# Attention expansions in two row groups and two banks, with a new bank plan for the eight slots

## The chip, the cores and the metric

The kernel is one program on one core of a Trainium2 chip. Its time is the device time of one execution in microseconds (us); less is better. The engines are TensorE (PE in the profile, with PEld for its weight loads), VectorE (DVE), ScalarE (ACT), GpSimd (POOL) and the queue that issues transfers (SP). PE writes only to PSUM, which has eight banks of 128 partitions by 512 fp32 columns; DVE and ACT read PSUM, POOL does not. Engines wait for each other by semaphores.

## The reference

```python
x = L0_attn_hidden_states                      # 16 x 256 x 128
x = x + 0.5 * ffn(layernorm(x))
x = x + retention(layernorm(x))
x = x + 0.5 * ffn(layernorm(x))

def ffn(src):                                  # 16 heads of 8 dimensions, 4 experts of 512
    q, k, v = src @ Wq + bq, src @ Wk + bk, src @ Wv + bv
    scores = einsum("bqhd,bkhd->bhqk", q, k) * 8 ** -0.5
    attn = einsum("bhqk,bkhd->bqhd", softmax(scores), v).reshape(B, T, 128) @ Wo + bo
    x = layer_norm(src + attn, ln1_g, ln1_b)
    expert_idx = remainder(floor(x @ router_w + router_b), 4)
    ff_out = W2[e] @ relu(W1[e] @ x + b1[e]) + b2[e] for the expert e of each token
    return layer_norm(x + ff_out, ln2_g, ln2_b)
```

The changed part is the attention inside `ffn`, which runs twice over 16 batch elements of 256 tokens.

## The kernel before

The program has five stages in a row: attention of the first `ffn`, its experts, the retention layer, attention of the second `ffn` (whose first iterations are woven into the last ones of retention), its experts. At the start a DMA also clears two DRAM tables of 17.5 MB each, into which POOL later writes rows (`sort_out`).

**An attention iteration `i`** (one batch element enters in each) is cut into eight slots, p = 0 to 7; every engine runs its own list of work slot by slot, written out by hand, and semaphores tie the lists together. A slot begins on PE with `score_burst`: eight matmuls that contract over 32 rows each (array shape 32*128 in the profile). Four are the scores of two heads of element `i` (line 540, into `score_duo`, banks 0 and 1), four are the shifted scores of two heads of an earlier group (line 546, into `prob_duo`, banks 2 and 3). Within a burst neighbours take different row groups and banks. DVE then takes the row maxima of `score_duo` (`maximum`, line 1251) and ACT the exponential of `prob_duo` (`exp`, line 970). There is one `score_duo` and one `prob_duo`, so the next burst waits for both (`max_done`, `exp_done`).

Behind the burst each slot has other work on PE:

- **expand(b, g)**, lines 526 to 535: 16 heads of 8 dimensions lie in four groups of 4 heads, that is 32 of the 128 partitions. An expansion spreads a group's query and key rows, kept as a rounded part `qk_hi` and a remainder `qk_lo`, into a stack of 32 rows for each head, by matmuls with 0/1 selectors `sel_r`. ACT copies query and key half to SBUF (`out_expand`, lines 955 and 956, about 0.38 and 0.48 us).
- **spread_max(b, g)**: adds the maxima to the query stack (lines 578, 580); ACT copies it (`shift_q`, line 962).
- **weigh_values(b, g)**: probabilities times values (line 596, array shape 128*32, 16 matmuls in the profile) into `pv_bank`, two groups side by side; ACT copies (`out_pv`, line 978).
- **att_to_tokens, att_to_dims, project_out**: transposes (605, 613) and the output projection (621), with `normalize` on DVE (1260, 1262), `out_attT` on ACT (985) and `add_attention` on DVE (1270) between them.
- **transposes, project_qk, project_v** for elements to come; DVE makes `qk_lo` (`split_qk`, line 1240).
- **position(b)**: small bf16 matmuls for the row numbers of the experts' table (630 to 633); DVE reads them in `place`.

Four banks serve all of this: `pv_bank` (bank 4) and the three rotating banks `a`, `b`, `c` (5, 6, 7). `take(which, reader, value)` waits until the last reader of that bank has finished and notes the next one. In the profile and in the order below a pair of banks is one tensor: duo2 is banks 4 and 5, duo3 is 6 and 7.

## Time and profile before

| | |
|---|---|
| median of 3 runs | 1073.31 us (1070.42 to 1078.86) |
| the profiled execution, device time | 1071.67 us |
| its span in the trace | 1069.9 us (1.8 us lie around it) |
| PE busy | 891.4 us, 83% |
| DVE busy | 761.7 us, 71% |
| ACT busy | 687.3 us, 64% |
| POOL busy | 618.9 us, 58% |
| first attention | about 13 to 310 us |
| experts | about 310 to 400 us |
| retention | about 400 to 670 us |
| second attention | about 670 to 960 us |
| experts | 960 to 1070 us |

Busy shares are means over stages with different limits. In a timeline row the first number is the start in us from the span's beginning, the second the time covered by the row's instructions, and brackets at the end give the idle time of that engine before it and what ended it; a row without brackets follows its predecessor closely. A matmul's row begins with the weight load that it needs, if nothing hides that.

### The profile page before, as it was taken

What the parts mean: (1) busy time and instruction counts of PE and PEld (TensorE: products, weight loads), DVE (VectorE), ACT (ScalarE), POOL (GpSimd) and SP (SyncE); (2) the same over time, 40 slices, a digit from 0 to 9 for tenths busy, and PEclk for the clock granted to TensorE, in tenths of its full rate; (3) what the DMA queues carried; (4) which work ended last, traced back from release to release, by engine and by line L of the source; (5) the groups of instructions that cost most, each with busy time, mean ns of one, the idle gap of its engine ahead of it and who ended that gap; (6) DMA issues with size and microseconds to landing.
All of it is one profiled execution on the core that took longest, in us unless ns stands there. A gap on an engine that the chain in (4) does not pass through costs nothing. (4 is left out here: it accounts for less than half of the span.)

```text
span 1069.9 us, 26869 instructions
## 1 busy us (share of the span) xinstructions
PE 891.4 (83%) x8603; PEld 662.6 (62%) x8603; DVE 761.7 (71%) x1900; ACT 687.3 (64%) x1402; POOL 618.9 (58%) x913
## 2 busy tenths in 40 slices
PE   5898999999957883788888888799999999975884
PEld 4566666666636883566666665666666666644884
DVE  4687888888864874465555655578888888873776
ACT  2586888888835772344343434488888888853764
POOL 4144657566572774366657666426575665652666
PEclk9898999999988996799999999799999999996998
DMA  9984991000017773000000000000000000006772
GB/s 307 411 328 56 367 405 45 10 20 10 21 36 216 245 221 94 1 1 1 0 0 0 0 0 1 1 2 12 11 20 10 20 15 15 22 20 195 213 215 89
DMA packets 41958, 97.70 MB, mean 91 GB/s; under 512 B 5240, under 2 KB 25486, under 8 KB 37276
## 3 DMA queue, kind: packets, MB, share of 16 engines
q1 hardware_dynamic: 36380, 84.16, 23.9%
q0 software_dynamic: 5504, 12.63, 3.3%
q8 instruction: 37, 0.61, 0.2%
q14 instruction: 37, 0.30, 0.1%
HBM read 44.68 MB, written 53.13 MB: 91 GB/s over the span
## 5 line engine op out<-in xcount | busy, mean ns | idle before, releaser
L1251 DVE TENSOR_REDUCE mx<-duo 128x4 fp32r<-128x1024 f32 x256 | 312.4, 1220 | 74.3 <-PE duo L540 69.4
L970 ACT ACTIVATE probs<-duo 128x1024 f32<-128x1024 f32 x256 | 263.2, 1029 | 54.1 <-PE duo L546 50.6
L540 PE MATMUL duo<-stacks 32*128 32x256 f32 x1024 | 133.7, 338 | 32.9 <-DVE mx L1251 26.8
L596 PE MATMUL duo<-probs,v_st 128*32 128x256 f32 x2048 | 140.9, 394 | 0.9 <-ACT probs L970 0.6
L1473 DVE TENSOR_TENSOR ret<-duo,dm 128x768 f32<-128x768 f32 x64 | 61.2, 957 | 104.2 <-PE duo L785 100.4
L546 PE MATMUL duo<-q_st,stacks 32*128 32x256 f32 x1024 | 131.2, 335 | 0.1
L540 PEld LDWEIGHTS duo<-stacks 32*128 32x128 f32 x1024 | 80.7, 191 | 68.9 <-issue 39.0
L1625 POOL TENSOR_TENSOR a_ln<-mv_ln,eps_ln 128x2 f32<-128x2 f32 x32 | 6.4, 199 | 145.8 <-DVE mv_ln L1216 145.8
L533 PE MATMUL duo<-qk_hi,sel_r 128*128 128x256 f32 x256 | 83.3, 345 | 7.4 <-DVE qk_lo L1240 7.4
L596 PEld LDWEIGHTS duo<-probs,v_st 128*32 128x32 f32 x2048 | 54.3, 111 | 42.2 <-issue 3.4
L546 PEld LDWEIGHTS duo<-q_st,stacks 32*128 32x128 f32 x1024 | 77.8, 188 | 1.4 <-ACT probs L970 0.5
L1678 POOL DMA_INDIRECT x_sorted<-rows,pos_all x64 | 66.2, 1034 | 19.0 <-issue 19.0
L677 PE MATMUL duo<-w,probs 128*128 x608 | 76.4, 280 | 0.4 <-issue 0.2
L677 PEld LDWEIGHTS duo<-w,probs 128*128 128x128 f32 x608 | 73.5, 197 | 0.8 <-issue 0.8
L1082 ACT ACTIVATE stacks<-duo 128x512 fp32r<-128x512 f32 x64 | 38.2, 598 | 54.7 <-PE duo L797 54.7
L962 ACT ACTIVATE q_st<-duo 128x256 fp32r<-128x256 f32 x128 | 49.6, 387 | 33.7 <-PE duo L580 33.7
L534 PE MATMUL duo<-qk_lo,sel_r 128*128 128x256 f32 x256 | 69.9, 293 | 0.0
L533 PEld LDWEIGHTS duo<-qk_hi,sel_r 128*128 128x128 f32 x256 | 50.9, 199 | 23.4 <-DVE qk_lo L1240 12.0
L956 ACT ACTIVATE stacks<-duo,small 128x256 fp32r<-128x256 f32 x128 | 61.8, 483 | 0.0
L1001 ACT ACTIVATE probs<-duo,wside 128x256 f32<-128x256 f32 x152 | 60.0, 470 | 1.8 <-PE duo L668 1.6
L1774 POOL TENSOR_TENSOR qk<-att_un 128x512 f32<-128x512 f32 x16 | 20.3, 1271 | 63.8 <-DVE att_un L1486 63.8
L955 ACT ACTIVATE stacks<-duo 128x256 fp32r<-128x256 f32 x128 | 49.2, 384 | 8.4 <-PE duo L534 8.2
(213 smaller groups left out, 2423.4 us busy)
## 6 DMA issues: line engine op xcount, KB each, us to landing
x_sorted<-ret SPq DMA_DIRECT2D x2, 17476.0 KB, 52.8
wbuf<-w_pack SPq DMA_DIRECT2D x38, 512.0 KB, 3.4
ret<-x_sorted SPq DMA_DIRECT2D x22, 257.0 KB, 3.5
stacks<-x_sorted SPq DMA_DIRECT2D x12, 257.0 KB, 3.7
wside<-w_pack SPq DMA_DIRECT2D x38, 66.0 KB, 4.0
w_pack<-wbuf SPq DMA_DIRECT2D x2, 1024.0 KB, 7.8
decay_rows<-prow SPq DMA_DIRECT2D x1, 1536.0 KB
probs<-x_sorted SPq DMA_DIRECT2D x4, 257.0 KB, 4.3
```

The source lines that it names most:

```text
L533: pe.matmul(half, sel_r[:, g, 2 * n, :], qk_hi[:, n, :], start=True, stop=False)
L534: last = pe.matmul(half, sel_r[:, g, 2 * n + 1, :], qk_lo[:, n, :], start=False, stop=True)
L540: return pe.matmul(score_bank[h % 2][:, t * SEQ:(t + 1) * SEQ], q_st[r:r + 32, g, t * P:(t + 1) * P], k_st[r:r + 32, g, :], start=True, st ...
L546: return pe.matmul(banks[h % 2][:, t * SEQ:(t + 1) * SEQ], k_st[r:r + 32, g, t * P:(t + 1) * P], q2_st[r:r + 32, g, :], start=True, stop=True)
L596: last = pe.matmul(pv_bank[32 * j:32 * j + 32, cols], v_st[:, t, h, :], probs[:, h % RING, t, :], start=(t == 0), stop=(t == TT - 1))
L677: last = pe.matmul(bank[4 + n % 2][:, t * P:(t + 1) * P], hid[:, n % 2, c, t * P:(t + 1) * P], w2[:, bass.ds(e * CPE + c, 1), :], start=(c ...
L956: act.activation(k_st[:, g, :], o[:, SEQ:2 * SEQ], ACT.Identity, bias=ones_col[:]).then_inc(ex_ready, 1)
L970: act.activation(probs[:, h % RING:h % RING + 2, :, :], duo_now[:].rearrange("p (n t q) -> p n t q", n=2, t=TT), ACT.Exp, scale=SCALE).the ...
L1001: act.activation(hid[:, n % 2, c, :], bank[c][:, 0:SEQ], ACT.Relu, bias=wside[:, n % 3, c:c + 1]).then_inc(h_ready, 1)
L1251: dve.tensor_reduce(rows, score_duo[:].rearrange("p (n t k) -> p n t k", n=2, t=TT), AX.X, ALU.max, negate=True).then_inc(max_done, 1)
L1473: dve.tensor_tensor(ret[:, 2 * g:2 * g + 2, :], both, dm[:, 2 * g:2 * g + 2, :], ALU.mult).then_inc(ret_ready, 1)
L1678: pool.indirect_dma_start(x_sorted[b // BATCH], bass.IndirectOffsetOnAxis(pos_all[:, b - base, t:t + 1], 0), rows[:, b - base, t, :], None ...
```

## The change

`expand` uses only the 32 rows of its group instead of all 128. Queries lie in row group g, keys (whose weight columns and bias are rolled by 32 on the host, and the key selectors with them) in row group g + 1, so that query and key matmuls can be in the array at once; they now write to different banks, query to `a`, key to `c`. The count of matmuls is the same, four for each expansion. `pv_bank` becomes a rotating bank `d`. `position` moves from slot 4 to slot 5, `att_to_dims` from slot 0 to slot 1, `place` steps one slot later. Which bank the other work takes is redone.

The core of the diff (left out are the same edits of `turn` at the start of a phase, and the packing of `vecs`):

```diff
-                        sel[p, g, kind, 32 * j + HD * part + d] = 1.0
+                        sel[(p + 32 * (kind // 2)) % P, g, kind, 32 * j + HD * part + d] = 1.0
...
+    A["Wk"], A["bk"] = np.roll(A["Wk"], 32, 1), np.roll(A["bk"], 32)
...
-                return {"a": bank_a, "b": bank_b, "c": bank_c}[which]
+                return {"a": bank_a, "b": bank_b, "c": bank_c, "d": pv_bank}[which]
...
-                o = take("caac"[g], ex_ready, b * 8 + 2 * g + 2)
-                for n in range(2):
-                    half = o[:, n * SEQ:(n + 1) * SEQ]
-                    pe.matmul(half, sel_r[:, g, 2 * n, :], qk_hi[:, n, :], start=True, stop=False)
-                    last = pe.matmul(half, sel_r[:, g, 2 * n + 1, :], qk_lo[:, n, :], start=False, stop=True)
+                o = take("a", ex_ready, b * 8 + 2 * g + 1), take("c", ex_ready, b * 8 + 2 * g + 2)
+                for m, part in enumerate((qk_hi, qk_lo)):
+                    for n in range(2):
+                        r = 32 * ((g + n) % GROUPS)
+                        last = pe.matmul(o[n][:, 0:SEQ], sel_r[r:r + 32, g, 2 * n + m, :], part[r:r + 32, n, :], start=(m == 0), stop=(m == 1))
...
-                o = take("aaca"[g], q2_ready, b * 4 + g + 1)
+                o = take("acac"[g], q2_ready, b * 4 + g + 1)
...
-                if g == 0:
-                    pe.wait_ge(va_ready, b + 1)
-                    wait(pe, un_ready, b * 2)
-                if g == 2:
-                    pe.wait_ge(vb_ready, b + 1)
-                    pe.wait_ge(un_ready, b * 2 + 1)
+                if g % 2 == 0:
+                    pe.wait_ge((va_ready, vb_ready)[g // 2], b + 1)
+                    take("d", un_ready, b * 2 + g // 2 + 1)
...
-                o = take("ba"[t], att_ready, b * 2 + t + 1)
+                o = take("db"[t], att_ready, b * 2 + t + 1)
...
-                o = take("c", attT_ready, b + 1)
+                o = take("a", attT_ready, b + 1)
...
-                o = take("c", y1_ready, b + 1)
+                o = take("d", y1_ready, b + 1)
...
-                            if live(i - 2, base):
-                                att_to_dims(i - 2)
                         elif p == 1:
                             if live(i - 1, base):
                                 weigh_values(i - 1, 1)
+                            if live(i - 2, base):
+                                att_to_dims(i - 2)
+                            if live(i - 1, base):
                                 spread_max(i - 1, 3)
...
                             if live(i - 1, base):
                                 weigh_values(i - 1, 2)
+                        elif p == 5:
                             if live(i - 3, base):
                                 position(i - 3)
-                        elif p == 5:
```

On PE, in slots 4 and 5 of an iteration with all its parts. Before, from the expansion behind the burst of slot 4 to the burst of slot 5:

```order
L533 MATMUL duo3<-qk_hi,sel_r 128x256 [waits y1_ready]
L534 MATMUL duo3<-qk_lo,sel_r 128x256
L533 MATMUL duo3<-qk_hi,sel_r 128x256
L534 MATMUL duo3<-qk_lo,sel_r 128x256
L596 MATMUL duo2<-probs,v_st 32x256 [waits un_ready,vb_ready,exp_done]
L596 MATMUL duo2<-probs,v_st 32x256 x7
L630 MATMUL duo2<-masks,tri_b 128x8 [waits q2_ready,router]
L631 MATMUL duo2<-masks,ones_b 128x4
L633 MATMUL duo2<-counts,ones_b 128x8 x2
L540 MATMUL duo0<-stacks 128x256 [waits exp_done,q2_ready,max_done]
```

The same place in the change, on to the small matmuls of `position` (now line 628) and the values of slot 5:

```order
L535 MATMUL duo2<-qk_hi,sel_r 128x256 [waits ex_ready,q2_ready]
L535 MATMUL duo3<-qk_hi,sel_r 128x256
L535 MATMUL duo2<-qk_lo,sel_r 128x256
L535 MATMUL duo3<-qk_lo,sel_r 128x256
L594 MATMUL duo2<-probs,v_st 32x256 [waits y1_ready,vb_ready,exp_done]
L594 MATMUL duo2<-probs,v_st 32x256 x7
L541 MATMUL duo0<-stacks 128x256 [waits exp_done,q2_ready,max_done]
L541 MATMUL duo0<-stacks 128x256
L547 MATMUL duo1<-q2_st,stacks 128x256 x2
L541 MATMUL duo0<-stacks 128x256 x2
L547 MATMUL duo1<-q2_st,stacks 128x256 x2
L628 MATMUL duo2<-masks,tri_b 128x8 [waits ex_ready,router]
```

The four matmuls of the expansion alternate between the two banks, and `position` stands behind the burst of slot 5, where it waits for ACT's query copy of slot 4 (`ex_ready`) instead of for `q2_ready`.

On DVE, in slots 5 and 6. Before, from the maxima of slot 5 to those of slot 6, with the row numbers' first step just ahead:

```order
L1314 TENSOR_TENSOR pos_f<-duo2,masks 128x8 [waits pos_ps]
L1251 TENSOR_REDUCE mx<-duo0 128x2x2 [waits score_ps,prep_ln]
L1240 SCALAR_TENSOR_TENSOR qk_lo<-duo3,bias_cols,qk_hi 128x256 [waits ex_ps,hi_ready]
L1240 SCALAR_TENSOR_TENSOR qk_lo<-duo3,bias_cols,qk_hi 128x256
L1318 TENSOR_REDUCE pos_all<-pos_f 128x2 [waits pos_ready]
L1320 TENSOR_TENSOR counts<-counts,masks 128x8
L1216 BN_AGGR mv_prep<-six_prep 128x2 x2
L1251 TENSOR_REDUCE mx<-duo0 128x2x2 [waits m_ps,score_ps]
```

In the change:

```order
L1254 TENSOR_REDUCE mx<-duo0 128x2x2 [waits score_ps,prep_ln]
L1317 TENSOR_TENSOR pos_f<-duo2,masks 128x8 [waits pos_ps]
L1243 SCALAR_TENSOR_TENSOR qk_lo<-duo3,bias_cols,qk_hi 128x256 [waits ex_ps,hi_ready]
L1243 SCALAR_TENSOR_TENSOR qk_lo<-duo3,bias_cols,qk_hi 128x256
L1219 BN_AGGR mv_prep<-six_prep 128x2 x2
L1254 TENSOR_REDUCE mx<-duo0 128x2x2 [waits m_ps,score_ps]
L1263 RECIPROCAL rsum<-duo2 128x16 [waits attT_ps,att_ps]
L1265 TENSOR_TENSOR att_pair<-duo2,rsum 128x128 [waits rsum_ready]
L1321 TENSOR_REDUCE pos_all<-pos_f 128x2 [waits pos_ready]
L1323 TENSOR_TENSOR counts<-counts,masks 128x8
```

The first step of the row numbers comes behind the maxima of slot 5 and ahead of `split_qk`; the other two come behind `normalize` in slot 6.

On ACT, in slots 0 and 1. Before:

```order
L956 ACTIVATE stacks<-duo2,small 128x256
L948 ACTIVATE v_nat<-duo3 128x256 [waits vb_ready,v_ps]
L985 ACTIVATE att_pair<-duo3 128x256 [waits wo_ps,attT_ps]
L970 ACTIVATE probs<-duo1 128x1024 [waits pv_done,prob_ps]
L978 ACTIVATE att_un<-duo2 128x512 [waits att_ps,pv_done]
L962 ACTIVATE q2_st<-duo2 128x256 [waits prob_ps,m_ps]
```

In the change:

```order
L958 ACTIVATE stacks<-duo3,small 128x256
L951 ACTIVATE v_nat<-duo3 128x256 [waits vb_ready,v_ps]
L972 ACTIVATE probs<-duo1 128x1024 [waits pv_done,prob_ps]
L980 ACTIVATE att_un<-duo2 128x512 [waits att_ps,pv_done]
L987 ACTIVATE att_pair<-duo2 128x256 [waits wo_ps,attT_ps]
L964 ACTIVATE q2_st<-duo3 128x256 [waits prob_ps,m_ps]
```

The copy of `att_to_dims` leaves slot 0 and stands in slot 1, ahead of the copy of the shifted queries.

## Rows read from the trace of the kernel before

**Rows 1.** The page, part 2: granted TensorE clock, tenths, 40 slices of the span.

```profile
PEclk9898999999988996799999999799999999996998
```

**Rows 2.** Busy time in stretches: PE, PEld, DVE, ACT, POOL with counts, PEclk, DMA.

```profile
114.00:131.00 17.00, 15.89 (x186) 11.05 (x187) 15.00 (x35) 14.54 (x28) 11.07 (x18) 1.00 1.03 413
...
898.00:915.00 17.00, 15.87 (x193) 10.98 (x185) 14.90 (x34) 14.59 (x28) 11.06 (x18) 1.00 0.04 15
```

**Rows 3.** Timeline, DVE: the maxima of slots 3 to 7 and 0 to 3.

```profile
239.65 1.21 DVE L1251 TENSOR_REDUCE mx<-duo 128x4 fp32r<-128x1024 f32 x1
...
241.92 1.23 DVE L1251 TENSOR_REDUCE mx<-duo 128x4 fp32r<-128x1024 f32 x1 [0.21 <-DVE six_ln L1210]
...
243.94 1.23 DVE L1251 TENSOR_REDUCE mx<-duo 128x4 fp32r<-128x1024 f32 x1 [0.27 <-PE duo L540]
...
246.16 1.19 DVE L1251 TENSOR_REDUCE mx<-duo 128x4 fp32r<-128x1024 f32 x1
...
248.09 1.23 DVE L1251 TENSOR_REDUCE mx<-duo 128x4 fp32r<-128x1024 f32 x1 [0.26 <-PE duo L540]
...
250.21 1.23 DVE L1251 TENSOR_REDUCE mx<-duo 128x4 fp32r<-128x1024 f32 x1 [0.40 <-PE duo L540]
...
252.39 1.22 DVE L1251 TENSOR_REDUCE mx<-duo 128x4 fp32r<-128x1024 f32 x1
...
254.38 1.23 DVE L1251 TENSOR_REDUCE mx<-duo 128x4 fp32r<-128x1024 f32 x1 [0.32 <-PE duo L540]
...
256.54 1.21 DVE L1251 TENSOR_REDUCE mx<-duo 128x4 fp32r<-128x1024 f32 x1
```

**Rows 4.** Timeline, PE: slots 4 and 5, to the burst of slot 6.

```profile
241.10 0.38 PE L540 MATMUL duo<-stacks 32*128 32x256 f32 x2 [0.39 <-DVE mx L1251]
...
241.32 0.28 PE L540 MATMUL duo<-stacks 32*128 32x256 f32 x2
...
241.53 0.39 PE L533 MATMUL duo<-qk_hi,sel_r 128*128 128x256 f32 x1
...
242.21 1.07 PE L596 MATMUL duo<-probs,v_st 128*32 128x256 f32 x16
...
243.21 0.18 PE L630 MATMUL duo<-masks,tri_b 128*128 128x8 bf16 x1
...
243.40 0.38 PE L540 MATMUL duo<-stacks 32*128 32x256 f32 x2
...
243.83 1.07 PE L596 MATMUL duo<-probs,v_st 128*32 128x256 f32 x16
...
244.83 0.38 PE L578 MATMUL duo<-stacks,ident_r 128*128 128x256 f32 x1
...
245.32 0.38 PE L540 MATMUL duo<-stacks 32*128 32x256 f32 x2
```

**Rows 5.** Timeline, ACT: query copy of slot 4, shifted-query copy of slot 5.

```profile
243.31 0.39 ACT L955 ACTIVATE stacks<-duo 128x256 fp32r<-128x256 f32 x1
...
245.47 0.38 ACT L962 ACTIVATE q_st<-duo 128x256 fp32r<-128x256 f32 x1
```

**Rows 6.** Timeline, PE and DVE: slot 6 from its expansion to the next burst.

```profile
246.00 0.39 PE L533 MATMUL duo<-qk_hi,sel_r 128*128 128x256 f32 x1 [0.18 <-DVE qk_lo L1240]
...
246.59 1.03 PE L605 MATMUL duo<-small,att_un 128*128 128x128 f32 x8
...
247.55 0.29 DVE L1262 TENSOR_TENSOR att_pair<-duo,rsum 128x128 f32<-128x128 f32 x1
...
247.55 0.38 PE L540 MATMUL duo<-stacks 32*128 32x256 f32 x2
```

**Rows 7.** Timeline, PE at the lower clock: an expansion and what follows it.

```profile
687.03 0.58 PE L533 MATMUL duo<-qk_hi,sel_r 128*128 128x256 f32 x1
...
688.05 1.89 PE L850 MATMUL duo<-wproj,hidden 128*128 128x128 f32 x8
```

**Rows 8.** Timeline, POOL: the first rows written to the cleared table.

```profile
94.95 1.23 POOL L1678 DMA_INDIRECT x_sorted<-rows,pos_all  x1 [3.09 <-issue]
```

More of the change, by code:

```diff
@@ L961, in shift_q @@
                 wait(act, prob_ps, (b - 1) * (NH // 2) + 2 * g + 2)
-                act.activation(q2_st[:, g, :], (bank_a, bank_a, bank_c, bank_a)[g][:, 0:SEQ], ACT.Copy).then_inc(q2_ready, 1)
+                act.activation(q2_st[:, g, :], (bank_a, bank_c)[g % 2][:, 0:SEQ], ACT.Copy).then_inc(q2_ready, 1)
             def exp(b, h, turned=None):
@@ L984, in out_attT @@
                 wait(act, wo_ps, b)
-                act.activation(attT[:], bank_c[:, 0:SEQ], ACT.Copy).then_inc(attT_ready, 1)
+                act.activation(attT[:], bank_a[:, 0:SEQ], ACT.Copy).then_inc(attT_ready, 1)
             def experts(ph):
@@ L1030, in body @@
                             out_v(i)
-                        if p == 0 and live(i - 2, base):
+                        if p == 1 and live(i - 1, base):
+                            out_pv(i - 1, 0)
+                        if p == 1 and live(i - 2, base):
                             out_attT(i - 2)
                         if p == 1 and live(i - 1, base):
-                            out_pv(i - 1, 0)
                             shift_q(i - 1, 3)
@@ L1449, in body @@
                                 normalize(i - 1, 0)
+                            if live(i - 3, base):
+                                place(i - 3, base, 1)
+                                place(i - 3, base, 2)
                         elif p == 7:
```

28 lines of the change are left out of this document (14 added, 14 removed).

## Prediction

> **What bounds the kernel now.** I read the clock line of the page first, then stretches of 17 us, then one iteration of the attention in order of time, engine by engine. The clock line shows that the two attention stages run at the full granted clock (2.4 GHz) nearly throughout; the digits 8 and 7 at the start of the first one and around the start of the second are stretches at half of it [rows 1]. In the first attention the 17 us windows from 114 to 284 us, ten of them, and in the second those from 745 to 915 us, another ten, all show the same picture: PE 15.9 of 17 us busy, DVE 14.8 to 15.0, ACT 14.5 [rows 2]. So a repeating iteration with three nearly full engines is what has to become shorter; no busy share alone says which of them sets its length.
>
> The maxima of `score_duo` are the thread through it, since each burst needs the maxima before it and each maximum needs its burst. Their starts give the iteration's length: 239.65 to 256.54 is 16.89 us for eight slots [rows 3]. The brackets sort the slots. Where the maxima have no bracket, or one that names DVE's own work (`six_ln`), DVE had been busy with its small jobs and set the pace: slot 3 to 4, 2.27 us; 5 to 6, 2.22; 0 to 1, 2.18; 2 to 3, 2.16; together 8.83 us. Where the bracket names PE, the burst came late: slot 4 to 5, 2.02 us; 6 to 7, 1.93; 7 to 0, 2.12; 1 to 2, 1.99; together 8.06 us. The shortest that such a slot can be is a loop of latencies: 1.23 us of maxima, 0.15 us from their end to the next burst (243.94 + 1.23 = 245.17, burst at 245.32) and 0.54 us from a burst to its maxima (243.40 to 243.94), 1.92 us [rows 3, 4]. Shorter PE work can therefore win at most 8.06 - 4 x 1.92 = 0.38 us of 16.89 in each iteration.
>
> **What the change does to one expansion.** Before, from its first matmul to the work behind it: 241.53 to 242.21, 0.68 us for four matmuls of full height [rows 4]. The new form has two steps of two matmuls in different row groups and banks. The nearest row is the burst: eight matmuls of 32 rows, four of them at 241.10 and four at 241.32, and the next work at 241.53, so two steps take 0.43 us even with four row groups at once [rows 4]. That is the upper end for the new expansion. Behind a burst it has the burst's array shape, so its first weight load can hide and the lower end is 0.22 us (one step each way of 0.11). An expansion saves 0.25 to 0.46 us of PE's time, four times in an iteration. After a wait, as in slot 6, I take 0.43; behind a burst, as in slot 4, either end, since it will not matter.
>
> The rows of full-height matmuls already follow each other closely although each needs its own weights in all row groups: the four take 0.68 us with the change of shape at the end, where weight loads in the open would double it [rows 4]. The Trainium skill says otherwise (TensorE: Matmul & The Clock Gate, Part 3, The mechanism): a weight load overlaps a running matmul only when its row group differs. By it the second pair here, which has the first pair's row groups, would load in the open, the expansion would take about 0.65 us and nothing would be saved; that is rival 3. The burst, whose second four also reuse the row groups of the first four, doesn't bear the rule out.
>
> **Slots 4 and 5.** Slot 4 is where PE is the limit: burst 241.10, expansion, values 242.21, `position` 243.21, burst 243.40 [rows 4]. The change takes 0.25 to 0.46 us off the expansion and 0.19 us by moving `position`. PE would be ready at 242.75 to 242.96, but the maxima of slot 4 end at 241.92 + 1.23 = 243.15 and the burst can't start before 243.30. Of some 0.5 us, 0.10 us reach the chain. Slot 5 gets the 0.19 us of `position`, and a new wait: bank `a` must have been read by ACT's query copy, done at 243.31 + 0.39 = 243.70, with a semaphore's 0.1 us 243.80 [rows 5], against 243.73 when PE would be there (243.30 + 0.43). Then `position` to 243.99, values to 244.99 (1.00 us as from 243.83 to 244.83), spread and burst of slot 6 at 245.48 (0.49 us as from 244.83 to 245.32) [rows 4]. Its maxima could start 0.54 us later, at 246.02; DVE's own work from slot 5 to 6 gives 243.84 + 2.22 = 246.06 (one small step added, two removed, about 0.04 us, not counted) [rows 3]. Before it was 246.16, so 0.10 us is still there, with PE and DVE level.
>
> **Slot 6.** The expansion before waited for `qk_lo` (246.00) [rows 6]. Now it also needs bank `c`, which ACT's shifted-query copy of slot 5 must have left: that copy began at 245.47 and begins 0.16 us later with the spread (244.99 for 244.83), so it ends at 246.01 and the expansion starts at 246.11 [rows 5]. With 0.43 us for it the transposes start at 246.54 in place of 246.59, and with their 0.96 us the burst of slot 7 at 247.50 in place of 247.55 [rows 6]; the maxima of slot 6 alone would allow 247.45. The gain shrinks to 0.05 us, 0.10 if the expansion is shorter.
>
> **The other slots.** In slot 7 the values now wait for `normalize` to leave bank `d`. It ends at 247.55 + 0.29 = 247.84, 0.49 us behind the maxima (246.16 + 1.19 = 247.35), so at 247.74 now; with 0.1 us for the semaphore 247.84, and the values can't come before 247.93 (burst 247.50 + 0.43) [rows 3, 6]: no cost, but 0.09 us from one. What is queued behind that wait is the values, the spread and the burst of slot 0. Slot 7's bound, values and spread on PE, is not touched. In slots 0 and 2 the expansion gets shorter under DVE's 2.18 and 2.16 us, worth nothing; the same cover hides the waits for both banks there, of which slot 2's stands behind ACT's moved copy (at most that copy's 0.4 us). If it did not, burst and maxima of slot 3 would be late by what exceeds 0.2 to 0.3 us. Slot 1 gets `att_to_dims` (two transposes, about 0.25 us) in place of slot 0. The bracket of 0.32 us before the maxima of slot 2 is the latency from the burst, and PE becomes about level with DVE: 0 to 0.1 us lost, I take 0 [rows 3].
>
> **The sum.** 0.05 to 0.10 us in an iteration, 0.07 taken, times 23 iterations (the twenty windows of 17 us [rows 2] hold 20 of 16.89 us, and I estimate three more at their edges) is 1.6 us. At the lower clock PE is the limit and an expansion takes 687.03 to 688.05, 1.02 us [rows 7]; half of it is saved. Two such expansions lie at the start of the second attention, this one and the one before it: 1.0 us. Those in the first 50 us win nothing, because POOL waits 3.09 us, until 94.95, for the cleared table, a transfer that takes its own time, and the iteration behind waits for POOL [rows 8]. Together 2.6 us: 1071.67 of the profiled execution becomes 1069.1, the median 1073.31 becomes 1070.7. I say 1070.
>
> **The rivals.**
> 1. **The whole cover is won.** All slots bound by PE fall to 1.92 us: 23 x 0.38 = 8.7 us, with start and clock stretches 2 more, 1063 us; 1062.6 is 1% less. For it: PE is the fullest engine [rows 2]. Against it: slot 7's PE work stays as it is, and slots 5 and 6 get new waits. 0.13.
> 2. **The new waits decide: slower.** The mechanism is the line `position` - values - spread - ACT copy - expansion - transposes in slots 5 and 6. From 246.06 for the maxima of slot 6 there is no slack: each 0.1 us on ACT's copies is 0.1 us for every iteration. If ACT's two copies and exponentials come one after another so that the copy of slot 5 is late by 0.4 us, an iteration is 0.35 us longer: 23 x 0.35 = 8 us, 1081 us; by 0.6 us 1086. It begins to cost when the copy is more than 0.05 us later than worked out. 0.15.
> 3. **The pairs don't overlap.** The expansion keeps its 0.68 us [rows 4]. Slots 4 and 5 still win 0.10 us, but slot 6 loses 0.11 + 0.06 us against now: an iteration is 0.1 us longer, 1075 us. 0.1.
> 4. **The clock.** PE has some 1 us less work in each iteration, and the grant could fall now and then, as where the digits are below 9 [rows 1]. At the lower clock a slot like that of slot 4 takes about 1 us more; one for each iteration gives 23 us, one in three 8 us, 1081 us. Against it: with PE busy 15.9 of 17 us the windows show 1.00, and 15 of 17 is not much less [rows 2]. 0.05.
> My forecast has 0.57.
>
> **The numbers.** Faster by over 1% (about what a measurement of this kernel can tell from no change is 1%) is rival 1 alone, 0.12. Slower by over 1%, above 1084, needs rival 2 or 4 at their far ends, 0.14 in all with what I have not seen. The rest is 0.74. The likeliest case has a range of its own of 1067 to 1074, from 0.05 to 0.2 us for an iteration and the spread of the three runs. The range over the cases runs from rival 1 (1063) to rival 2 (1081).
>
> **What the changed profile would show.** Right: the four matmuls of an expansion start in two pairs about 0.1 us apart, and PE's busy time in a 17 us window falls from 15.9 by 0.5 to 1 us; DVE's and ACT's stay; the maxima repeat after 16.8 us; the burst of slot 5 is bracketed by DVE; the expansion of slot 6 starts behind ACT's line 964. Wrong: a bracket of over 0.5 us before the values of slot 7 or the expansions of slots 2 and 6; equal spacing of the four matmuls; clock digits under 9 between 114 and 284 us; or an iteration below 16.6 us.

## The result and the profile after

The changed kernel takes 1091.13 us (median of four runs, 1088.83 to 1101.93) against 1074.26 us (1070.42 to 1078.86). The ratio is 1.0175, 95% interval [1.0096, 1.0254]: slower, by some 17 us. I had said 1070, within 1%. Here and in all that follows, executions of a kernel that lie over 1.5% above its fastest count as a slower state and are left out of means, clocks and ratios (the table at the end of the experiments has how many count). The profiled execution after took 1090.87 us; the one of before took 1071.67.

The first lines of the page after (the second is the granted TensorE clock in 40 slices) and the row of the score matmuls with TensorE's idle time in front of them:

```profile
span 1089.1 us, 26885 instructions
...
PEclk9998999999878996899999999699999999866997
...
L541 PE MATMUL duo<-stacks 32*128 32x256 f32 x1024 | 136.0, 343 | 54.0 <-DVE mx L1254 46.4
```

Against [rows 1] the clock line is lower at the end of the first attention (8 for 9, then 7 for 8), at the end of the second (8 and 6 for two 9s) and at the very end (7 for 8), and PE waits 46.4 us for DVE's maxima, 26.8 before. One iteration in the middle of the first attention, from DVE's timeline after (start, duration, then line, operation and tile; the bracket is idle time and what ended it); it is the iteration of [rows 3], 0.60 us earlier:

```profile
241.32 1.23 DVE L1254 TENSOR_REDUCE mx<-duo 128x4 fp32r<-128x1024 f32 x1 [0.21 <-DVE six_ln L1213]
...
243.15 1.23 DVE L1254 TENSOR_REDUCE mx<-duo 128x4 fp32r<-128x1024 f32 x1 [0.44 <-PE duo L541]
...
245.47 1.23 DVE L1254 TENSOR_REDUCE mx<-duo 128x4 fp32r<-128x1024 f32 x1
246.61 0.25 DVE L1263 RECIPROCAL rsum<-duo 128x16 f32<-128x16 f32 x1
246.89 0.29 DVE L1265 TENSOR_TENSOR att_pair<-duo,rsum 128x128 f32<-128x128 f32 x1
247.11 0.16 DVE L1321 TENSOR_REDUCE pos_all<-pos_f 128x8 f32 x1
247.19 0.67 DVE L1323 TENSOR_TENSOR counts<-counts,masks 128x8 bf16<-128x8 bf16 x1
247.78 1.21 DVE L1254 TENSOR_REDUCE mx<-duo 128x4 fp32r<-128x1024 f32 x1
...
249.88 1.23 DVE L1254 TENSOR_REDUCE mx<-duo 128x4 fp32r<-128x1024 f32 x1 [0.40 <-PE duo L541]
...
258.52 1.23 DVE L1254 TENSOR_REDUCE mx<-duo 128x4 fp32r<-128x1024 f32 x1 [0.21 <-DVE six_ln L1213]
```

The iteration is 258.52 - 241.32 = 17.20 us; between the same slots before it was 16.90. Slot 4 to 5 is 1.83 us (2.02 before), 5 to 6 is 2.32 (2.22), 6 to 7 is 2.31 (1.93), and the other five are within 0.04 us of what they were. The maxima behind slot 6 (247.78) have no bracket: DVE is busy throughout, and its smallest job, the addition of `counts` (128 x 8 numbers), takes 0.67 us. What POOL does at the time, from its timeline after:

```profile
247.11 0.73 POOL L1669 TENSOR_TENSOR rows<-xs,vecs_sb 128x256 f32<-128x256 f32 x1
247.79 0.46 POOL L1651 TENSOR_TENSOR v_st<-v_nat,ones_wide 128x128 f32<-128x128 f32 x1
```

`own_row` (L1669) ends at 247.84, `counts` at 247.86. The matmuls of the slots that the change is about, from PE's timeline after:

```profile
242.61 0.38 PE L541 MATMUL duo<-stacks 32*128 32x256 f32 x2 [0.37 <-DVE mx L1254]
...
243.17 0.18 PE L628 MATMUL duo<-masks,tri_b 128*128 128x8 bf16 x1
...
245.45 0.39 PE L535 MATMUL duo<-qk_hi,sel_r 32*128 32x256 f32 x2
245.67 0.28 PE L535 MATMUL duo<-qk_lo,sel_r 32*128 32x256 f32 x2
245.88 1.09 PE L603 MATMUL duo<-small,att_un 128*128 128x128 f32 x8
246.91 0.38 PE L541 MATMUL duo<-stacks 32*128 32x256 f32 x2
```

The expansion of slot 6 is two pairs and takes 0.43 us to the transposes. So the edit on PE does what it was said to do; other things cost the time. Where they lie shows in matched events of the two profiled executions (after minus before):

| event | before | after | difference |
|---|---|---|---|
| maxima, start of the first attention's middle part | 103.48 | 100.76 | -2.7 |
| maxima, between nine and ten iterations later | 266.90 | 266.81 | -0.1 |
| last maxima of the first attention | 297.17 | 299.66 | +2.5 |
| maxima, second attention, middle | 830.69 | 837.25 | +6.6 |
| maxima, second attention, ahead of its last iteration | 931.53 | 939.60 | +8.1 |
| POOL's first `a_ln` behind the second attention | 952.29 | 967.74 | +15.5 |
| end of the span | 1069.9 | 1089.1 | +19.2 |

Two kinds of loss: some 0.3 us for each iteration of the middle, and steps at the ends of the attentions. At the steps the clock is lower than before. The end of the second attention in stretches, before (us; then busy time and instructions of PE, PEld, DVE, ACT, POOL; then granted clock, DMA share, GB/s):

```profile
940.00:948.00 8.00, 7.57 (x100) 4.65 (x92) 6.68 (x16) 6.03 (x10) 6.32 (x10) 1.00 0.00 0
948.00:956.00 8.00, 6.79 (x82) 4.05 (x79) 2.81 (x15) 5.88 (x9) 4.24 (x7) 1.00 0.11 35
```

and after:

```profile
940.00:948.00 8.00, 6.67 (x78) 4.68 (x79) 7.15 (x16) 6.90 (x14) 1.38 (x2) 0.90 0.11 37
948.00:956.00 8.00, 8.00 (x64) 4.63 (x63) 4.03 (x10) 4.36 (x7) 5.05 (x8) 0.50 0.00 0
956.00:964.00 8.00, 7.42 (x56) 4.12 (x56) 3.63 (x14) 3.92 (x5) 2.26 (x3) 0.50 0.10 35
```

0.50 is the lower of the two levels, 1.2 GHz. From 948 to 964 us PE runs at half clock and is nearly always busy, and by POOL's `a_ln` 7.4 us more are lost (+8.1 to +15.5). The first slow matmuls come at 946.80 us, behind a gap of 0.88 us in which PE waits for the maxima:

```profile
946.80 0.58 PE L541 MATMUL duo<-stacks 32*128 32x256 f32 x2 [0.88 <-DVE mx L1254]
```

The same slot of the same iteration has such a gap in the first attention, and the clock falls there too, at 291.0 us:

```profile
290.64 0.38 PE L541 MATMUL duo<-stacks 32*128 32x256 f32 x2 [0.88 <-DVE mx L1254]
```

Before, the gap of that slot is a little shorter, and the clock stays at 1.00 behind it:

```profile
938.72 0.38 PE L540 MATMUL duo<-stacks 32*128 32x256 f32 x2 [0.78 <-DVE mx L1251]
```

The last 3.7 us of the table are lost behind the attention, in the experts, where the change edits nothing; the clock is at its lower level there for 39 us in place of 35. Why these stages are slower as well stays open.

### The profile page after: what moved, and what is told of

The parts are those of the page before. It is cut to its first block and busy times, and to the rows that moved or that the text cites. A ratio compares the mean times of both kernels' runs of the same rounds, so it can differ in the third digit from the quotient of the medians.

```text
span 1089.1 us, 26885 instructions
## 1 busy us (share of the span) xinstructions
PE 887.2 (81%) x8603; PEld 638.9 (59%) x8603; DVE 772.0 (71%) x1900; ACT 691.9 (64%) x1402; POOL 619.9 (57%) x913
## 5 line engine op out<-in xcount | busy, mean ns | idle before, releaser
L541 PE MATMUL duo<-stacks 32*128 32x256 f32 x1024 | 136.0, 343 | 54.0 <-DVE mx L1254 46.4
L594 PE MATMUL duo<-probs,v_st 128*32 128x256 f32 x2048 | 148.9, 412 | 1.5 <-ACT probs L972 1.4
L547 PE MATMUL duo<-q_st,stacks 32*128 32x256 f32 x1024 | 134.3, 343 | 0.1
L547 PEld LDWEIGHTS duo<-q_st,stacks 32*128 32x128 f32 x1024 | 80.1, 194 | 1.3 <-ACT probs L972 0.3
L1651 POOL TENSOR_TENSOR v_st<-v_nat,ones_wide 128x128 f32<-128x128 f32 x64 | 30.7, 481 | 41.4 <-PE duo L594 41.4
L1637 POOL TENSOR_SCALAR s_nat<-xs,mv_prep,rstd_prep 128x128 f32<-128x128 f32 x64 | 50.5, 791 | 6.5 <-POOL rstd_prep L1630 6.4
L579 PE MATMUL duo<-stacks,ident_r 128*128 128x256 f32 x128 | 53.9, 421 | 0.1
L535 PE MATMUL duo<-qk_hi,sel_r 32*128 32x256 f32 x256 | 48.2, 361 | 6.4 <-DVE qk_lo L1243 2.7
```

The lines of the kernel that those rows point to most:

```text
L541: return pe.matmul(score_bank[h % 2][:, t * SEQ:(t + 1) * SEQ], q_st[r:r + 32, g, t * P:(t + 1) * P], k_st[r:r + 32, g, :], start=True, st ...
L547: return pe.matmul(banks[h % 2][:, t * SEQ:(t + 1) * SEQ], k_st[r:r + 32, g, t * P:(t + 1) * P], q2_st[r:r + 32, g, :], start=True, stop=True)
L579: pe.matmul(o[:, 0:SEQ], ident_r[:], q_st[:, g, :], start=True, stop=True)
L594: last = pe.matmul(pv_bank[32 * j:32 * j + 32, cols], v_st[:, t, h, :], probs[:, h % RING, t, :], start=(t == 0), stop=(t == TT - 1))
L1637: pool.tensor_scalar(dst(t), src(t), s["mv"][:, t, 0:1], s["rstd"][:, t:t + 1], ALU.subtract, ALU.mult).then_inc(done, 1)
```

## The experiments

Two theories for the iteration. **A**: `counts`, with two inputs in SBUF, is held up by POOL's instruction beside it. **B**: the new waits for ACT's copies (my rival 2). Two for the clock. **C**: the new expansion lowers the granted clock. **D**: chance, or something else. Times of a run below are means over the executions that count, beside the mean of the kernel before in the same hour on the same chip; the clock is the mean over the same executions. The ratio is that of the measurement, with its 95% interval; it is not the quotient of the two means and can differ from it by some 0.3% (1081.1 / 1073.0 is 1.0076 where the ratio is 1.0094).

### The place steps

Back to slot 5, in the changed kernel (`e1_back`):

```diff
@@ slot 5 of DVE
                             if live(i + 1, base):
                                 split_qk(i + 1)
+                            if live(i - 3, base):
+                                place(i - 3, base, 1)
+                                place(i - 3, base, 2)
@@ slot 6
                                 normalize(i - 1, 0)
-                            if live(i - 3, base):
-                                place(i - 3, base, 1)
-                                place(i - 3, base, 2)
```

> The changed kernel with place steps 1 and 2 (pos_all, counts) moved back from slot 6 to slot 5, behind split_qk; all else as changed. Theory A (counts, two SBUF inputs on DVE, is held up by POOL's own_row beside it, 0.67 us for 0.15): counts takes 0.15 us again, slot 6 to 7 falls from 2.31 to about 1.85 us, slot 5 to 6 grows from 2.32 to about 2.45, an iteration is 16.8 to 16.9 us for 17.19, and the time falls by 23 x 0.33 = 7.6 us to about 1083 us; the low clock at the end of both attentions stays. Theory B (the new waits for ACT's copies in slots 5 and 6 set the iteration): still 17.2 us for an iteration and 1090 us.

Measured: iteration 16.84 us (241.08 to 257.92), 1081.1 us against 1073.0, ratio 1.0094 [1.0049, 1.0138]. DVE's timeline of slots 5 to 7:

```profile
244.91 0.15 DVE L1321 TENSOR_REDUCE pos_all<-pos_f 128x8 f32 x1
244.97 0.15 DVE L1323 TENSOR_TENSOR counts<-counts,masks 128x8 bf16<-128x8 bf16 x1
...
245.22 1.23 DVE L1254 TENSOR_REDUCE mx<-duo 128x4 fp32r<-128x1024 f32 x1
...
247.21 1.23 DVE L1254 TENSOR_REDUCE mx<-duo 128x4 fp32r<-128x1024 f32 x1 [0.27 <-PE duo L541]
```

`counts` takes 0.15 us again, although POOL is busy beside it, with two `TENSOR_SCALAR` instructions of one tensor input:

```profile
243.72 1.57 POOL L1637 TENSOR_SCALAR token_bufs<-token_bufs,mv_ln,rstd_ln 128x128 f32<-128x128 f32 x2 [0.18 <-POOL rstd_ln L1630]
```

These last to 245.29, `counts` from 244.97 to 245.12. Slot 6 to 7 is 1.99 us, with PE in the bracket. I had 1.85 for it and 2.45 for slot 5 to 6, which stays at 2.31: the two small steps fit into time in which DVE would otherwise have waited for the burst. The iteration is now 0.06 us shorter than before the change, as predicted for it, and still the kernel is slower. In the changed kernel the two steps no longer stand there, and 5 to 6 takes as long (2.32). So A holds for this kernel, B falls, and something else costs some 8 us.

The same steps moved in the kernel before, alone (`e2_place`):

```diff
@@ before, slot 5 of DVE
-                            if live(i - 3, base):
-                                place(i - 3, base, 1)
-                                place(i - 3, base, 2)
@@ slot 6
                                 normalize(i - 1, 0)
+                            if live(i - 3, base):
+                                place(i - 3, base, 1)
+                                place(i - 3, base, 2)
```

> The kernel before with one part of the change alone: place steps 1 and 2 moved from slot 5 to behind normalize in slot 6. Theory A: POOL's own_row (0.73 us, from 247.72 in the trace of before) lies on counts, which takes 0.5 to 0.7 us for 0.15; slot 6 to 7 grows from 1.93 to about 2.3 us, slot 5 to 6 loses up to 0.15; an iteration of about 17.1 to 17.2 us for 16.90, and 1078 to 1081 us. Theory B: two steps of 0.15 us change place, 16.9 us and 1073 us. Under both PE keeps its full-height expansions, so the clock at the end of the attentions stays at 1.00 and its 12 us are not lost.

Measured: iteration 17.19 us (243.26 to 260.45), the whole 0.29 us from this edit alone. 1076.2 us against 1073.0, ratio 1.0021 [0.9978, 1.0064]. The iteration is what A said. The time is lower than the 1078 to 1081 us worked out, and its interval reaches no change: 0.29 us times 22 iterations is 6.4 us, inside the scatter of single executions. POOL and DVE in slot 6, from the timeline:

```profile
249.04 0.74 POOL L1666 TENSOR_TENSOR rows<-xs,vecs_sb 128x256 f32<-128x256 f32 x1
...
249.15 0.64 DVE L1320 TENSOR_TENSOR counts<-counts,masks 128x8 bf16<-128x8 bf16 x1
```

`own_row` ends at 249.78, `counts` at 249.79. Only one of the two steps moved on, to slot 7, in the changed kernel (`e3_counts`; the line `place(i - 3, base, 2)` goes from behind `normalize(i - 1, 0)` to behind `normalize(i - 1, 1)`):

> The changed kernel with counts alone (place step 2) moved from slot 6 to slot 7, behind the second normalize; pos_all stays in slot 6. Theory A: in slot 7 POOL is at its tick and its indirect DMA, so counts takes 0.15 us; slot 6 to 7 is about 1.85 to 1.9 us for 2.31, slot 7 to 0 stays at 2.10 since PE sets it; an iteration is 16.7 to 16.8 us, shorter than 16.90 of before, and the time about 1080 us (23 x 0.45 = 10 us less than the changed kernel). Theory B: 17.2 us and 1090 us. If instead any small step behind normalize is what costs, half of the 0.38 us stays and an iteration is 17.0 us.

Measured: iteration 16.84 us (241.37 to 258.21), slot 6 to 7 1.99 us, `counts` 0.15 us in slot 7 with `pos_all` left in slot 6. 1081.1 us against 1073.0, ratio 1.0069 [1.0021, 1.0117]. It is `counts` alone, and not any small step behind `normalize`. The forecast of slot 6 to 7, 1.85 to 1.9 us, was too short here as in `e1_back`: without the held `counts` the bracket names PE, and the slot stays at 1.99.

The last test leaves DVE's order alone and moves POOL's instruction (`e7_ownrow`, a single execution):

```diff
                     elif live(i - 2, base):
+                        own_row(i - 2, base)
                         rstd(i - 2, "ln1")
                         ...
                         make_x1(i - 2, base)
-                        own_row(i - 2, base)
```

> The changed kernel with one POOL instruction moved: own_row (two SBUF inputs, 0.73 us), which lies on counts from 247.1 to 247.8, goes to the front of POOL's ln1 chain, where POOL idles 4.9 us. DVE's order is untouched. Theory A: counts then stands beside POOL's next instruction with two SBUF inputs, the second place_v (0.46 us), which moves up to about 247.1; counts ends with it, so takes 0.3 to 0.45 us for 0.67, and slot 6 to 7 falls from 2.31 to 2.0 to 2.1 us. If counts is slow for a reason of its own (bf16, or the normalize ahead of it), it keeps 0.67 us and slot 6 to 7 its 2.31.

Measured: `counts` 0.38 us, slot 6 to 7 2.02 us, iteration 16.86 us (239.84 to 256.70), 1077.5 us with a clock of 0.928. POOL and DVE, from its timeline:

```profile
245.61 0.46 POOL L1651 TENSOR_TENSOR v_st<-v_nat,ones_wide 128x128 f32<-128x128 f32 x1
...
245.70 0.38 DVE L1323 TENSOR_TENSOR counts<-counts,masks 128x8 bf16<-128x8 bf16 x1
```

`counts` now ends at 246.08 and `place_v` at 246.07. In three kernels `counts` ends when POOL's instruction does, whichever that is and whenever it ends. The Trainium skill has the rule (SBUF — State Buffer, Who interferes with whom): a VectorE instruction with two inputs in SBUF contends with a GpSimd instruction that reads SBUF, and the one that comes second waits for the whole of the first. These traces agree for POOL's instructions with two tensor inputs: 0.67, 0.64 and 0.38 us for `counts`, which takes 0.15 us otherwise. Beside the `TENSOR_SCALAR` of `e1_back`, which reads SBUF too, it does not wait: there the rule says more than these traces bear out. POOL instructions of other kinds than these two were not tried.

Does the bank plan need these moves at all? With `position` and the place steps where they were, in slots 4 and 5 (`e8_pos4`: the changed kernel with those lines of PE and DVE as before):

> The changed kernel with position in slot 4 and place steps 0, 1 and 2 in slots 4, 5, 5 as before: what is left of the change is the expansion, the banks and att_to_dims in slot 1. Slot 4 to 5 stays at about 1.83 us (PE gets 0.19 us more there, under 0.45 us of waiting for its own burst's latency; at worst 1.9), slot 5 to 6 falls from 2.31 to 2.2, slot 6 to 7 is 1.9 to 2.0: 16.7 to 16.85 us for an iteration. By theory C' the clock stays at 0.92 to 0.93 and the time at 1078 to 1082 us, above the 1074 of before although every iteration is shorter; if the clock were not tied to the expansion it would be 1070 us.

Measured: iteration 17.67 us, 1093.8 us against 1072.4, ratio 1.0187 [1.0135, 1.0239], mean clock 0.9275. A miss: I had 16.7 to 16.85 us. ACT, PE and DVE in slot 4, from the timeline:

```profile
250.25 0.39 ACT L957 ACTIVATE stacks<-duo 128x256 fp32r<-128x256 f32 x1
...
250.70 0.18 PE L628 MATMUL duo<-masks,tri_b 128*128 128x8 bf16 x1 [0.92 <-ACT stacks L957]
...
251.00 0.17 DVE L1317 TENSOR_TENSOR pos_f<-duo,masks 128x8 f32<-128x8 f32 x1 [0.76 <-PE duo L631]
```

`position` shares bank `a` with the expansion just ahead of it and waits 0.92 us for ACT to read it, with the burst of slot 5 behind it. So with these banks, and ACT's work in this order, `position` and place step 0 belong in slot 5. Steps 1 and 2 need not go to slot 6, as `e1_back` shows. Part of the longer iteration is `counts` again, which takes 0.47 us in slot 5 of this run.

### The clock

First, more work for PE at the place where the clock fell, in the last iteration of each attention (`e4_twice`):

```diff
-                for m, part in enumerate((qk_hi, qk_lo)):
+                for m, part in enumerate((qk_hi, qk_lo, qk_hi, qk_lo) if isinstance(b, int) and b % BATCH == BATCH - 1 and g else (qk_hi, qk_lo)):
+                    m %= 2
```

> The changed kernel, but in the last iteration of each attention expansions 1 to 3 are multiplied twice (the second pass writes the same result over the first): 0.43 us more of TensorE work in slots 0, 2 and 4 of two iterations, where PE idled 0.2 to 0.9 us. Theory C (the granted clock falls at the end of both attentions because the shorter expansions leave PE too idle there): the clock stays at 1.00 behind these slots as it does in the kernel before, and the time falls by 10 to 12 us to about 1080 us. Theory D (the low clock there is chance or comes from elsewhere): the clock falls as in the changed kernel, 1090 us or slightly more. An iteration in the middle stays at 17.19 us under both.

Measured: 1090.6 us against 1073.0, ratio 1.0196 [1.0123, 1.027], mean clock 0.9213 over four executions. The stretch from 280 to 310 us of its profile has 0.94; the changed kernel has 0.89 in its first profile and 0.94 in its second (`e0_again`). The clock did not come back; by this run alone I would have dropped theory C.

Then the expansion itself, at full height again, in `e1_back` (`e5_full`, the sums and the new banks unchanged, `sel` and `Wk` without the roll):

```diff
-                        r = 32 * ((g + n) % GROUPS)
-                        last = pe.matmul(o[n][:, 0:SEQ], sel_r[r:r + 32, g, 2 * n + m, :], part[r:r + 32, n, :], start=(m == 0), stop=(m == 1))
+                        last = pe.matmul(o[n][:, 0:SEQ], sel_r[:, g, 2 * n + m, :], part[:, n, :], start=(m == 0), stop=(m == 1))
```

> Run e1_back (changed kernel, place steps 1 and 2 back in slot 5) with its expansions at full height again: four matmuls over 128 dimensions into the new banks a and c, sel and Wk without the roll. Over all runs so far the span follows the mean granted clock of its run with -0.93 us for each 0.001, and the kernels with the new expansion run at 0.919 to 0.926, those with the old one at 0.936 and 0.937. Theory C' (it is the new expansion, with less work for TensorE, that lowers the granted clock): the mean clock is back at 0.935 to 0.938 and the time about 1072 to 1075 us, although each expansion takes 0.68 us for 0.43. Theory E (the bank plan and its waits shift the clock's stretches, not the expansion): the clock stays near 0.925 and the time is 1081 us or more. Iteration in the middle 16.85 to 16.95 us under both.

Measured: 1070.7 us against 1072.4, ratio 0.9993 [0.9952, 1.0033], mean clock 0.9423, iteration 16.93 us. As theory C says, with the height back the clock is back. Only six of the ten executions count here; over all ten the mean is 1075.4 us and the clock 0.9376, still that of the kernel before (1072.4 us, 0.9367). The same undone in the changed kernel as it is (`e10_height`), beside that kernel once more in the same hour (`e0_again`):

> The changed kernel with one part undone: expansions at full height (four matmuls over 128 dimensions, sel and Wk without the roll); banks and place steps stay as changed. If the clock follows the height of the expansions and the two losses add up, the mean clock is back at 0.935 to 0.938 and only the longer iteration (17.2 us, counts at 0.67 us in slot 6) is left: 1078 to 1083 us. If the clock's loss came from the place steps or the banks instead, the clock stays at 0.92 and the time at 1090 us.

> The changed kernel as it is, on the chip and in the hour of its variants: mean clock 0.918 to 0.922, 1088 to 1094 us; an iteration of 17.19 us.

Measured: `e10_height` 1082.4 us, ratio 1.0048 [1.0014, 1.0081], clock 0.9366; `e0_again` 1095.8 us, ratio 1.0225 [1.0162, 1.0288], clock 0.9187; before 1076.5 us, clock 0.935. The iteration of `e0_again` is 17.18 us, and in `e10_height` slot 5 to 6 is 2.32, 6 to 7 2.30 and `counts` 0.59 us. This splits the loss: 1082.4 - 1076.5 = 5.9 us for the place steps, 1095.8 - 1082.4 = 13.4 us for the height, 19.3 us in all. The split depends on the order in which the parts are undone. Against the kernel before of its own hour each of the four kernels stands at:

| | steps 1 and 2 in slot 5 | in slot 6 |
|---|---|---|
| full height | -1.7 us (e5_full) | +5.9 us (e10_height) |
| 32 rows | +8.1 us (e1_back) | +19.3 us (e0_again) |

The height costs 9.8 or 13.4 us, the steps 7.6 or 11.2 us. By the intervals of the ratios each corner is uncertain by 4 to 7 us, and `e0_again` has only three executions that count; so both parts are there, but which is the larger is not measured.

Is it PE's busy time, or the height? `e6_warm` is `e1_back` with expansions 1 and 2, under DVE's cover, multiplied twice in all iterations, still 32 rows high (the condition in the `for` of `e4_twice` is `g in (1, 2)`):

> Run e1_back with expansions 1 and 2 (slots 0 and 2, where DVE sets the pace) multiplied twice in every iteration, the second pass over the first, still in row groups of 32: 0.86 us more of TensorE busy time in an iteration, about the 1.0 us that the change took away. Theory C' in the form 'busy time counts': the mean clock is back at 0.935 or more with an iteration of 16.85 us, so 1070 to 1073 us. In the form 'rows of the array count' (a matmul of 32 rows works a quarter of the array, one of 128 rows all of it): the clock stays near 0.926 and the time at 1080 us or above, while e5_full has its clock back.

Measured: 1085.8 us against 1072.4, ratio 1.0136 [1.0065, 1.0208], clock 0.9268, iteration 17.0 us (the longer expansion is not wholly covered: slot 2 to 3 grows from 2.16 to 2.29). The stretches of its profile, at the end of the first attention and in its middle:

```profile
280.00:310.00 30.00, 26.81 (x338) 17.27 (x338) 22.94 (x59) 24.95 (x42) 16.32 (x26) 1.00 0.06 20
...
114.00:131.00 17.00, 16.09 (x195) 10.74 (x194) 15.06 (x35) 14.79 (x28) 9.38 (x16) 1.00 1.03 406
```

PE is busier than before the change (16.09 of 17 us against 15.89 [rows 2]), the end of the first attention has its full clock in this profile, and yet the mean clock of the four executions stays where `e1_back` has it. Adding work in the small form does not bring the clock back; the expansion's height is the edit that does.

Where is the clock lost? Full height in slots 0 and 2 alone, in all iterations (`e9_mixed`: rows `slice(0, P) if g in (1, 2) else slice(r, r + 32)`):

> Run e1_back with expansions 1 and 2 (slots 0 and 2, where DVE sets the pace) at full height again, and 0 and 3 (slots 6 and 4, where PE does) in row groups of 32. If the height of the expansions in the steady iterations is what the granted clock follows, the mean clock lies between 0.926 (e1_back) and 0.938 (e5_full), about 0.932, an iteration is 16.84 us and the time 1074 to 1077 us, near the kernel before. If only the expansions in slots 4 and 6 matter for the clock (they stand beside PE's waits), it stays at 0.926 and 1080 us.

Measured: 1078.3 us against 1076.5, ratio 1.0021 [0.9979, 1.0063], clock 0.9366. By these numbers half of the height would give back all of the clock, more than I had allowed. But only seven of the twelve executions count; over all twelve the mean is 1082.2 us and the clock 0.9288, against 1077.5 us and 0.9341 of the kernel before, which is between the two forms. So how much of the clock it gives back stays open. Full height in the first and last iterations of each attention alone, all four expansions, and 32 rows in the ten of the loop (`e11_ends`, the condition is `isinstance(b, int)`, which holds outside the hardware loop):

> Run e1_back with full-height expansions in the first and last iterations of each attention (those outside the hardware loop, some 8 of 18), and expansions of 32 rows in the ten iterations of the loop. In the profiles of the runs so far the granted clock is 1.00 in the middle of both attentions with either height; from 280 to 310 us it is 1.00 in the five profiles with full-height expansions and 0.89 to 0.94 in six of the eight with 32 rows. If the clock is lost at the ends, by the expansions there, the mean clock is back at 0.934 to 0.938, the stretch from 280 to 310 us shows 1.00, and with an iteration of 16.84 us in the loops the time is 1072 to 1076 us, no more than the kernel before. If the loop's expansions lower it too (in executions that the profiles don't show, or later, in the ends behind the loop), the clock stays at 0.926 to 0.930 and the time is 1080 us.

Measured: 1072.9 us against 1072.5, ratio 1.000 [0.9951, 1.0049], clock 0.9393, iteration 16.84 us. Over all twelve executions the clock is 0.9364, 0.9256 in `e1_back`. The stretch from 280 to 310 us in the profiles of `e11_ends`, `e5_full`, `e1_back` and the changed kernel, in this order (the last column but two is the clock):

```profile
280.00:310.00 30.00, 26.43 (x313) 17.37 (x311) 21.63 (x56) 23.20 (x38) 16.98 (x26) 1.00 0.06 20
```

```profile
280.00:310.00 30.00, 24.69 (x288) 15.84 (x280) 21.81 (x60) 20.88 (x34) 16.65 (x26) 1.00 0.07 22
```

```profile
280.00:310.00 30.00, 25.87 (x295) 15.90 (x293) 20.51 (x54) 21.26 (x35) 16.22 (x26) 0.94 0.06 19
```

```profile
280.00:310.00 30.00, 26.56 (x291) 16.19 (x292) 19.91 (x50) 22.01 (x36) 14.69 (x24) 0.89 0.06 19
```

So the expansions outside the loop, at the starts and ends of the attentions, are enough to decide the mean clock; the ten in the middle can have 32 rows without a measurable loss. That the clock is lost only at the ends does not follow, and the fourteen profiles say otherwise. Of the eight with 32 rows throughout, six have time at the lower level in the last 30 us before the last maxima of an attention (`e6_warm` and `e8_pos4` have none), and none of the other six has any there. But these places hold little of the difference. Mean time at the lower level in a profile, in us:

| stage | full throughout (4 profiles) | 32 rows throughout (8) |
|---|---|---|
| first attention, up to its last 30 us | 12.8 | 17.1 |
| its last 30 us | 0 | 3.8 |
| experts and retention | 70.8 | 74.7 |
| second attention, first 60 us | 11.9 | 20.0 |
| its middle | 0 | 1.7 |
| its last 30 us | 0 | 3.4 |
| behind its last maxima | 31.5 | 40.7 |
| together | 127.0 | 161.4 |

The ends have 7 of the 34 us, the start of the second attention 8, and what follows the last maxima 9. Single executions differ by as much, so the table is a hint and no measurement.

| kernel | expansion | `counts` in | iteration, us | executions that count | mean clock | ratio to before |
|---|---|---|---|---|---|---|
| before | full | slot 5 | 16.90 | 13 to 21 an hour | 0.935 to 0.939 | 1 |
| e2_place | full | slot 6 | 17.19 | 8 of 10 | 0.9395 | 1.0021 |
| e10_height | full, new banks | slot 6 | 17.2 | 10 of 10 | 0.9366 | 1.0048 |
| e5_full | full, new banks | slot 5 | 16.93 | 6 of 10 | 0.9423 | 0.9993 |
| e11_ends | full outside the loop | slot 5 | 16.84 | 8 of 12 | 0.9393 | 1.000 |
| e9_mixed | full in slots 0, 2 | slot 5 | 16.85 | 7 of 12 | 0.9366 | 1.0021 |
| e1_back | 32 rows | slot 5 | 16.84 | 10 of 10 | 0.9256 | 1.0094 |
| e3_counts | 32 rows | slot 7 | 16.84 | 8 of 10 | 0.9246 | 1.0069 |
| e6_warm | 32 rows, two of four doubled | slot 5 | 17.0 | 4 of 4 | 0.9268 | 1.0136 |
| e7_ownrow | 32 rows | slot 6 | 16.86 | 1 | 0.928 | |
| e4_twice | 32 rows, doubled in the last iterations | slot 6 | 17.2 | 4 of 4 | 0.9213 | 1.0196 |
| e8_pos4 | 32 rows | slot 5 | 17.67 | 4 of 4 | 0.9275 | 1.0187 |
| the change | 32 rows | slot 6 | 17.2 | 4 of 4, 3 of 4 | 0.9188, 0.9187 | 1.0175, 1.0225 |

No version here is measurably faster than the kernel before. The best of them wins 0.06 us in an iteration, some 1.3 us in all, which is less than these measurements can tell.

## Why the prediction was wrong

**PE's part was right, slot by slot.** On the clock of [rows 3] (0.60 us added) the maxima of slot 6 come at 246.07 (I had 246.06), the expansion of slot 6 at 246.05 (246.11), the transposes at 246.48 (246.54) and the burst of slot 7 at 247.51 (247.50). `position` waited for ACT's query copy and the expansion of slot 6 for the shifted one, as written, and neither cost anything. The values of slot 7 started 0.43 us behind the burst, not held by `normalize`. PE's busy time from 114 to 131 us fell from 15.89 to 15.01, DVE's and ACT's stayed. The 0.07 us that I took for an iteration is the 0.06 us of `e1_back`. For slot 4 to 5 I had 0.10 us of gain and it was 0.19; DVE's steps in slot 5 took it back.

**The step that failed** is the sentence "one small step added, two removed, about 0.04 us, not counted", and what it leaves out: the two that are removed from slot 5 go to slot 6, and I never priced slot 6 with them in it. I looked there for PE's burst (247.50, so maxima at 248.04); the maxima came at 248.38 on the same clock, because DVE was not free. Even at 0.15 us each the two steps had to be added to DVE's chain of slot 6. Their real price, 0.5 us more, needed POOL's row beside DVE's: [rows 5, 6] show ACT, PE and DVE there, and I looked at POOL only for the cleared table. Size: 0.35 us an iteration (17.19 against 16.84) in the changed kernel, 7.7 us in 22 such iterations; in the time the steps cost 5.9 us with full height, and more, up to 11.2 us, with 32 rows, where the clock falls as well (0.9256 to 0.9187).

**The clock was in the rivals with 0.05, and costs as much again: 10 to 13 us.** It is the second step that failed. The argument against it, that 15 of 17 us is not much less than 15.9, was right for the middle: nineteen of the twenty windows of 17 us stayed at 1.00, one (762 to 779 us) has 0.90. But the rival was priced for the middle only. The end of an attention, where the next iterations have no more expansions and transposes to give and PE waits 0.78 us in one slot, and the start of the second, where [rows 1] already show a 7, are places where it was lost. The sign to look for that I named, digits under 9 between 114 and 284 us, would have missed it. And the mechanism I gave, less work for PE, isn't what the runs bear out: `e6_warm` gives PE more work and has no better clock. It is the height, for a reason that stays open.

**The other rivals.** Rival 1 (the whole cover) was false: no iteration fell below 16.84 us. Rival 2 had the sign, but not for its reason: the line through ACT's copies held. What it describes is seen in `e8_pos4`, where a wait for ACT's copy does stand on the path, for 0.92 us. Rival 3 was false: behind a burst the pairs start 0.12 us apart, and an expansion takes 0.33 us there and 0.43 behind a wait.

**The start.** I wrote that the first 50 us win nothing, because POOL waits for the cleared table. In this profile they won 2.7 us. Up to 60 us its clock is at the lower level for 3.4 us, before it was 10.2; in `e0_again`, the same kernel with 10.2 us as before, the gain is 1.3 us, so some half of the 2.7 us is luck with the clock. The rest could be won because POOL's wait moved along with its start. Its first row, after:

```profile
92.05 1.23 POOL L1681 DMA_INDIRECT x_sorted<-rows,pos_all  x1 [3.18 <-issue]
```

It is 2.9 us earlier than in [rows 8], with 3.2 us ahead of it. In the fourteen profiles it starts at 92.1 to 95.0 us, always with a wait of 3.0 to 3.8 us, so that time goes with the path there and is not the end of a transfer that takes its own time. The 2.7 us were used up by the longer iterations by 266 us.

## What to carry to other kernels

When a change moves small instructions of one engine, list what each other engine has beside them in the new place, with the inputs of both: an addition of 8 numbers in each partition that is free beside one instruction of POOL costs half a microsecond beside another. When a change takes work from TensorE, look for its price in clock not only in the full middle but in the thin places, where iterations run in and out; here it was enough to keep the larger form of the expansion there (`e11_ends`). And measure the parts apart: here the edit that the change is about won in the timeline and lost in the time.

## What the runs showed of the hardware

- A VectorE addition with both inputs in SBUF stood still until the GpSimd instruction beside it had ended: 0.67, 0.64 and 0.38 us in place of 0.15, each ending within 0.02 us of it. That holds beside GpSimd instructions with two tensor inputs; beside one with a single input (1.57 us for two, in `e1_back`) it took its 0.15 us. In `e8_pos4` an addition of `make_x1` does the same to `counts` in slot 5 (0.47 us).
- The granted clock of a run followed the height of a few matmuls. Kernels whose expansions were 128 rows high, throughout or outside the loop, had means of 0.935 to 0.942; those with 32 rows throughout 0.919 to 0.928, and `e6_warm`, with more of the small matmuls, is among them (0.9268). Single executions overlap (up to 0.933 with 32 rows, down to 0.929 with full height). Why the clock tells the two apart no run here shows.
- Full-height matmuls that each load their own weights follow each other without the loads in the open: 0.12 us from one to the next. The four of an expansion take 0.68 us where the values, of another array shape, follow [rows 4], and 0.59 us where full-height transposes follow [rows 6]. Their order makes no difference: as two pairs in two banks they take 0.67 us ahead of the values (245.83 to 246.50 in `e10_height`) and 0.58 us ahead of the transposes:

```profile
250.35 0.50 PE L533 MATMUL duo<-qk_hi,sel_r 128*128 128x256 f32 x2
250.69 0.40 PE L533 MATMUL duo<-qk_lo,sel_r 128*128 128x256 f32 x2
250.93 1.04 PE L601 MATMUL duo<-small,att_un 128*128 128x128 f32 x8
```

So the 32-row form saves 0.35 us of PE's time in slot 4 (0.68 to 0.33), but only 0.16 us in slot 6 (0.59 to 0.43), less than the 0.25 us that the prediction had as the least for an expansion; its times for slot 6 were right because it took them from the rows of slot 6.
